# Laying the second pass's buffers in layers over the first's in a two-pass attention and FFN kernel, and interleaving the work at the seam

## What is computed

```python
xn = _layernorm(x)
Q, K = elu(xn @ Wq + bq) + 1, elu(xn @ Wk + bk) + 1
KV = einsum('bshd,bshm->bhdm', K, v)
Z = 1 / (einsum('bshd,bhd->bsh', Q, K.sum(axis=1)) + EPS)
o = einsum('bshd,bhdm,bsh->bshm', Q, KV, Z)
x1 = _layer_norm(xn + o @ Wo + bo, g1, be1)
s = _layer_norm(x1 + gelu(x1 @ W1 + b1) @ W2 + b2, g2, be2)
h = silu(fp4_linear(xn, w_gate)) * fp4_linear(xn, w_up)
out = x + s * silu(fp4_linear(h, w_down))
```

## Time and profile before

| | us |
|---|---|
| median of 3 runs | 1816.92 (1813.23 to 1817.27) |
| the profiled execution, its own time | 1815.74 |
| its span, first to last instruction | 1813.9 |
| TensorE, VectorE, ScalarE, GpSimd busy | 1708.1, 1334.5, 969.1, 705.6 |
| chain that ended last, by engine | PE 76%, DVE 13%, issue 4%, DMA 2%, ACT 2% |

### The profile page before, as it was taken

How to read it: one execution, slowest core, us unless ns; L and a number is a source line. 1 busy time by engine, 2 the same in 40 slices (tenths; PEclk the granted TensorE clock), 3 DMA queues, 4 the chain that set the end, 5 groups by cost and what they waited for, 6 DMA issues and landing times.

```text
span 1813.9 us, 30486 instructions
## 1 busy us (share of the span) xinstructions
PE 1708.1 (94%) x11091; PEld 1515.0 (84%) x11091; DVE 1334.5 (74%) x2733; ACT 969.1 (53%) x1756; POOL 705.6 (39%) x518
## 2 busy tenths in 40 slices
PE   6888999999869999999999999999999999999997
PEld 4766778787659988898998989899898998989886
DVE  5575645646357879797787879788787978878794
ACT  5444555555334654646465464646556464655543
POOL 4443433333213434333434434343343334334344
PEclk9899999999979999999999999999999999999998
DMA  5311222312130010111101010110101021010100
GB/s 175 115 69 54 81 92 69 117 61 100 55 131 1 1 48 1 48 45 53 48 1 48 1 47 23 75 48 1 48 1 47 2 96 48 1 48 1 47 1 24
DMA packets 65946, 89.33 MB, mean 49 GB/s; under 512 B 4211, under 2 KB 50439, under 8 KB 64774
## 3 DMA queue, kind: packets, MB, share of 16 engines
q1 hardware_dynamic: 65798, 87.39, 14.2%
HBM read 53.29 MB, written 34.08 MB: 48 GB/s over the span
## 4 chain that ended last, share of the span: by engine, by line
PE 76%; DVE 13%; issue 4%; DMA 2%; ACT 2%; POOL 1%; SPq 1%; POOLq 0%; DVEq 0%; ACTq 0%
PE QH L77 9%; PE QH L79 9%; PE QH L78 9%; PE AC L77 8%; PE AC L79 8%; PE AC L78 8%; PE GU L77 4%; PE GU L79 4%; PE GU L78 4%; PE QH L696 2%; PE DN L77 2%; PE DN L79 2%; PE DN L78 2%; PE TT L778 2%; DVE hb L1655 1%
## 5 line engine op out<-in xcount | busy, mean ns | idle before, releaser
L2102 POOL TENSOR_TENSOR hb<-hb,rs_h 128x704 f32<-128x704 f32 x64 | 89.0, 1391 | 322.4 <-DVE rs_h L1662 322.4
L1115 ACT ACTIVATE rh<-QH 128x512 fp32r<-128x512 f32 x256 | 150.3, 595 | 103.5 <-DVE QH L1790 101.9
L1805 DVE TENSOR_TENSOR rl<-QH,rh 128x512 fp32r<-128x512 f32 x128 | 85.2, 675 | 131.0 <-ACT rh L1115 103.6
L77 PE MATMUL GU<-wgh,xqh 128*128 128x352 f32 x448 | 148.4, 331 | 6.8 <-DVE hb L1655 5.2
L2107 POOL TENSOR_TENSOR hb<-hb,sn_h 128x704 f32<-128x704 f32 x64 | 89.1, 1392 | 165.1 <-DVE hb L1667 165.1
L1415 DVE SCALAR_TENSOR_TENSOR u<-ex,QH 128x512 f32<-128x512 f32 x128 | 84.9, 682 | 91.9 <-ACT ex L986 91.3
L77 PE MATMUL AC<-Mh,rh 128*128 128x256 f32 x512 | 146.5, 286 | 0.0
L78 PE MATMUL GU<-wgl,xqh 128*128 128x352 f32 x448 | 145.7, 325 | 0.0
L79 PE MATMUL GU<-wgh,xql 128*128 128x352 f32 x448 | 145.4, 324 | 0.0
L77 PE MATMUL AC<-w2h,rh 128*128 128x256 f32 x512 | 144.6, 282 | 0.0
L79 PE MATMUL AC<-Mh,rl 128*128 128x256 f32 x512 | 143.9, 281 | 0.0
(11 more groups left out here) (232 smaller groups left out, 5724.4 us busy)
## 6 DMA issues: line engine op xcount, KB each, us to landing
xa<-in_L_attn_src SPq DMA_DIRECT2D x16, 512.0 KB, 4.7
xt_scratch<-xth SPq DMA_DIRECT2D x32, 256.0 KB, 4.9
xt_scratch<-xtl SPq DMA_DIRECT2D x32, 256.0 KB, 5.0
xb<-in_L_attn_src SPq DMA_DIRECT2D x16, 512.0 KB, 4.1
xnTh<-xt_scratch SPq DMA_DIRECT2D x32, 256.0 KB, 4.6
xnTl<-xt_scratch SPq DMA_DIRECT2D x32, 256.0 KB, 5.4
out<-x SPq DMA_DIRECT2D x16, 512.0 KB, 6.5
m_scratch<-mh SPq DMA_DIRECT2D x16, 256.0 KB, 2.4
```

The costliest lines, as they stand in the source:

```text
L77: e.matmul(outp, lh, rh, start=start, stop=False, skip_group_check=check)
L1115: e.activation(RH[j % 4][:], src, ACT.Copy).then_inc(S[sem], 1)
L1805: e.tensor_tensor(RL[j % 4][:], QH[:, (j % 2) * 512:(j % 2 + 1) * 512], f(RH[j % 4][:]), ALU.subtract).then_inc(S["gel"], 1)
L2102: e.tensor_tensor(hb, hb, spread(rs_h[i % 2][:], 44), ALU.mult).then_inc(S["hin"], 1)
```

## The change

Nothing that is computed changes. The edits:

1. **Buffers.** The one scope A becomes three layers. The row buffers Xb[0], XN and the small am_x, sn_x, rs_x get bytes that only rawc and vrows used. xnTh, xnTl and xa (and dn_s, zhi) lie over `raw`, the buffer of the weight chain. The rest of the prologue's buffers (zd, sel, XC, HC, xqh, Q32, EG, HB, ksB, Mh, ...) lie over the buffers of the tiles. Those of the maps (gt, kvt, wo_s, mhl, ...) lie under Xb[1], x1, xTh, Gb, RH, RL, hqh. So `end_of_a` becomes three waits: `raw_done`, `main_done`, `maps_done`.
2. **Loads.** `load_xb(0)`, `load_xn(0)` and the six loads of row vectors go to tile 50 of SyncE's loop, behind `raw_done`. `load_m(0)` follows `main_done`, ahead of the stores of the last maps.
3. **Group 0's first steps.** `x_norm(0, 0..3)` go to ScalarE's tiles 58 to 61, `x_max` and `x_scale` of both pairs to VectorE's tiles 60 and 62, `x_in(0, 0)` to GpSimd's tile 61.
4. **The last maps** are written between the first Q products on TensorE, ScalarE and VectorE, all in bank DN (before, DN and TT in turn).
5. **GpSimd.** `x_plus_bo(0)` goes from ahead of `h_in(0)` to behind `h_out(1)` and `maps_done`.
6. **Weights' chain.** The parts 2 and 3 are quantised at tiles 26 and 28 (before, 14 and 20). Their turns are at 30 to 33 and 42 to 45 (before, 25 to 32). rawc no longer shares gt.
7. The loop's turn for g = 0 is written out, in the same order, and the loop begins at 1.

```diff
-        turn_at = {**{14 + n: n for n in range(4)}, **{25 + n: 4 + n for n in range(8)}}
-        quant_at = {10: 0, 12: 1, 14: 2, 20: 3}
+        turn_at = {14: 0, 15: 1, 16: 2, 17: 3, 30: 4, 31: 5, 32: 6, 33: 7, 42: 8, 43: 9, 44: 10, 45: 11}
+        quant_at = {10: 0, 12: 1, 26: 2, 28: 3}
...
+        def main_done(w):
+            w.wait_ge(S["A_G"], 2 * NT)
+            w.wait_ge(S["A_K"], 2 * NT)
+            w.wait_ge(S["A_xl"], NT)
+            w.wait_ge(S["xs0"], 32 * (NT // 4))
+            w.wait_ge(S["xs1"], 32 * (NT // 4))
+        def maps_done(w):
+            w.wait_ge(S["A_ksm"], NB)
+            w.wait_ge(S["A_M"], 4 * NB)
+            w.wait_ge(S["A_Mc"], 8 * NB)
+            w.wait_ge(S["A_mh"], 4 * NB)
+            w.wait_ge(S["A_ml"], 4 * NB)
+            w.wait_ge(S["A_ks"], 5 * NB)
+            w.wait_ge(S["kst"], 16 * NB)
+            w.wait_ge(S["m0"], 32 * 2 * NB)
+            w.wait_ge(S["m1"], 32 * 2 * NB)
+        def raw_done(w):
+            w.wait_ge(S["A_wT"], 12)
+            w.wait_ge(S["A_qp"], 4)
```

SyncE:

```diff
-                if i == 34:
+                if i == 50:
+                    raw_done(w)
+                    load_xb(0)
+                    load_xn(0)
...
-            w.wait_ge(S["A_k"], 2 * NT)
-            w.wait_ge(S["A_K"], 2 * NT)
-            e.dma_start(Xb[0][:], src_t[0]).then_inc(S["x0"], 16)
+            main_done(w)
+            load_m(0)
...
-            end_of_a(w)
...
-            load_xn(0)
-            load_m(0)
+            maps_done(w)
```

TensorE:

```diff
+            q_proj(0, 0)
             k_sums(NB - 1)
             kv_map(NB - 1, 0)
+            q_proj(0, 1)
             kv_map(NB - 1, 1)
-            for r in range(4):
-                m_map(NB - 1, r)
-            end_of_a(w)
...
-            q_proj(0, 0)
-            q_proj(0, 1)
             q_proj(0, 2)
             q_proj(0, 3)
+            m_map(NB - 1, 0)
+            m_map(NB - 1, 1)
             turn_xq(0, 0)
             q_proj(0, 4)
             q_proj(0, 5)
+            m_map(NB - 1, 2)
             gate_up(0, 1)
+            m_map(NB - 1, 3)
             q_proj(0, 6)
             q_proj(0, 7)
             gate_up(0, 0)
```

VectorE (ScalarE likewise: `m_hi` 0 to 3 between the `q_exp`, `maps_done` ahead of `z_hi(0, 0)`):

```diff
-            x_max(0, 0)
-            x_scale(0, 0)
+            k_sums(NB - 1)
             q_elu(0, 0)
             x_round(0, 0)
+            kv_out(NB - 1, 0)
             q_elu(0, 1)
-            x_max(0, 1)
+            kv_out(NB - 1, 1)
             q_elu(0, 2)
+            m_out(NB - 1, 0)
             q_elu(0, 3)
-            x_scale(0, 1)
+            m_lo(NB - 1, 0)
+            m_out(NB - 1, 1)
             xq_lo(0, 0)
+            m_lo(NB - 1, 1)
             q_elu(0, 4)
+            m_out(NB - 1, 2)
             q_elu(0, 5)
             x_round(0, 1)
+            m_lo(NB - 1, 2)
+            m_out(NB - 1, 3)
             gate_mul(0, 1)
+            m_lo(NB - 1, 3)
```

GpSimd:

```diff
-            end_of_a(w)
+            main_done(w)
...
-            x_in(0, 0)
             x_out(0, 0)
             x_in(0, 1)
             x_out(0, 1)
-            x_plus_bo(0)
             h_in(0)
             h_out(0)
             h_in(1)
             h_out(1)
+            maps_done(w)
+            x_plus_bo(0)
             ln1_rstd(0, 0)
```

More of the change, by code:

```diff
@@ new lines, in turn_h @@
+            def turn_h(i, hf):
+                g, t = i // 4, i % 4
+                w.wait_ge(S["hout"], i + 1)
+                w.wait_ge(S["hb0"], 3)
+                w.wait_ge(S["hTh"], 2 * i + hf)
+                w.wait_ge(S["hTl"], 2 * i + hf)
+                n = 2 * g + (3 if t == 3 and g + 1 < NG else 2)
+                w.wait_ge(S["xqTh"], n)
+                w.wait_ge(S["xqTl"], n)
+                for k in range(3):
+                    c = hf * HALF + k * 128
+                    last = e.transpose(TT[:, k * 128:(k + 1) * 128], HB[i % 3][:, c:c + 128], ident[:])
+                last.then_inc(S["hT"], 1)
@@ L1894, in _ @@
             gelu_lo(0, 5)
-            for g in range(NG):
+            gelu_lo(0, 6)
+            h_round(3)
+            h_lo(2, 0)
+            x_max(1, 0)
+            x_scale(1, 0)
+            gelu_lo(0, 7)
+            q_elu(1, 0)
+            x_round(1, 0)
+            q_elu(1, 1)
+            h_lo(2, 1)
+            g_mul(1)
+            ln_add("lnb", 0, 0)
+            ln_add("lnb", 0, 1)
+            x_max(1, 1)
+            q_elu(1, 2)
+            q_elu(1, 3)
+            x_scale(1, 1)
@@ new lines, in _ @@
+            ln_stats("lnb", 0)
+            xq_lo(1, 0)
+            q_elu(1, 4)
+            q_elu(1, 5)
+            x_round(1, 1)
+            g_mul(2)
+            gate_mul(4, 1)
+            q_elu(1, 6)
+            h_lo(3, 0)
+            q_elu(1, 7)
+            gate_mul(4, 0)
+            h_max(4)
+            den_inverse(1)
+            h_lo(3, 1)
+            z_parts(1)
+            gate_mul(5, 0)
+            h_scale(4)
+            gate_mul(5, 1)
+            xq_lo(1, 1)
+            z_mul(1, 0)
@@ new lines, in _ @@
+            z_mul(1, 1)
+            z_lo(1, 0)
+            z_lo(1, 1)
+            h_max(5)
+            z_mul(1, 2)
+            z_mul(1, 3)
+            gate_mul(6, 1)
+            z_lo(1, 2)
+            z_lo(1, 3)
+            h_round(4)
+            z_mul(1, 4)
+            z_mul(1, 5)
+            g_mul(3)
+            z_lo(1, 4)
+            z_lo(1, 5)
+            h_scale(5)
+            z_mul(1, 6)
+            z_mul(1, 7)
+            h_lo(4, 0)
+            z_lo(1, 6)
+            z_lo(1, 7)
@@ new lines, in _ @@
+            gate_mul(6, 0)
+            h_round(5)
+            h_lo(4, 1)
+            ln1_add(1, 0)
+            ln1_stats(1, 0)
+            ln1_add(1, 1)
+            ln1_stats(1, 1)
+            ln1_norm(1, 0)
+            ln1_norm(1, 1)
+            gate_mul(7, 0)
+            h_lo(5, 0)
+            xT_half(1, 0, "x1T", "x1Th", "x1Tl")
+            xT_half(1, 1, "x1T", "x1Th", "x1Tl")
+            final_add(0)
+            g_mul(4)
+            gate_mul(7, 1)
+            h_lo(5, 1)
+            h_max(6)
@@ L2174, in _ @@
             h_out(2)
-            for g in range(NG):
+            x_in(1, 0)
+            x_out(1, 0)
+            h_out(3)
+            x_in(1, 1)
+            ln_rstd("lnb", 0)
+            x_out(1, 1)
+            x_plus_bo(1)
+            h_in(4)
+            x2_affine(0)
+            h_out(4)
+            h_in(5)
+            final_mul(0)
+            h_out(5)
+            ln1_rstd(1, 0)
+            ln1_rstd(1, 1)
+            h_in(6)
+            h_in(7)
+            x1_residual(1)
+            h_out(6)
+            for g in range(1, NG):
                 a, b, c, d = 4 * g, 4 * g + 1, 4 * g + 2, 4 * g + 3
```

1078 lines of the change are left out of this document (605 added, 473 removed).

## The result

The changed kernel takes 1794.52 us (median of four runs, 1789.76 to 1800.31) against 1817.10 for the kernel before (four runs, 1813.23 to 1817.39): ratio 0.9882, 95% interval 0.9849 to 0.9915. A second measurement gave 1796.44 against 1814.49, ratio 0.9904 (0.9887 to 0.9921). So 18 to 23 us are gone. The forecast was 1801.5 within 1794 to 1810: the sign and the range hold, but the time lies at the low end.

A forecast was written before the change was run, and what follows sets the result against it. TensorE, nearly always busy in both passes, was taken to bound the kernel. 1815.7 - 22.4 + 0.5 + 3.1 + 1.5 + 2 = 1800.4; with the median 1.2 above the profiled execution, 1801.5 us, range 1794 to 1810.

The forecast's parts named there:

- The seam: Between the two passes: early rows and last maps laid between Q products, about 29.2 us from 478.7, gain 22.4.
- my layout: Step-by-step order of TensorE's work between the passes, from 478.7 until gate_up(0, 0) ends at about 508.1, before 530.5.
- x_plus_bo(0): GpSimd step behind h_out(1): ln1_add(0, 0) starts 3.1 us later, uncovered; +3.1, and +1.5 for the clock.
- The first rival: At turn_x1(0, 0): TensorE has the 3.1 us to spare, x_plus_bo is covered, total 1797; chance 0.15.
- The chain: Weights' turns and quantising in the first pass: 6 to 8 us go, 8 to 10 come, net +2 (-4 to +7).
- The mechanism: First pass: two consecutive turns stall TensorE when no K product lies between them; 3.18 us at tile 16's turn.
- The rival of 1827.5: First pass: VectorE and GpSimd fall behind at tiles 26 to 33 and 42 to 45, K comes late; chance 0.03.
- The collision at tiles 28 and 29: VectorE and GpSimd share a port pair: quant_round(2) at tile 29 waits for quant_in(3), an estimated 1.3 us more.
- Group 0's first steps: Steps moved to the end of the first pass lie mostly in idle ScalarE and VectorE time; 0 to 1 us, taken as +0.5.
- what would make the forecast wrong: First pass growing by more than 10 us, or new SBUF places changing an instruction's duration, for which no reason was seen.

The follow-up runs named there:

- the first pair: Changed kernel against the same with x_plus_bo(0) back ahead of h_in(0); the latter took 1790.66 us, ratio 0.9868 to the kernel before.
- the faster kernel: Changed kernel with x_plus_bo(0) ahead of h_in(0), turns spaced so none follows another without a K product between, part 3 quantised at tile 30: 1778.12 us, ratio 0.9813.

## Why the prediction came out as it did

**The seam: right, 28.6 us for 29.4.** Gain 51.8 - 28.6 = 23.2 instead of 22.4. The order was read off step by step: k_sums ended within 0.1 of its place after 478.7, kv_map(0) took 3.65 for the 3.4 of the lower clock that I had kept, m_map(1) waited 0.96 for the 0.9, gate_up(0, 0) waited 0.40 for VectorE. Taking back the early load loses 10.5 of it, taking back the interleaving 11.9. (The last step of my layout, 505.9 plus a gate_up of 1.9, gives 507.8 and not 508.1; it changes nothing.) maps_done opened early enough: the last store of the maps was issued at 512.19 and SyncE's load behind it at 515.11, and TensorE had no wait that traces to it.

**x_plus_bo(0): the wait right, the price right.** 3.50 for the 3.4, no cover. With the clock behind it I had 3.1 + 1.5 = 4.6. By the medians it was 5.8 and 2.4 when undone in the new layout, and 4.5 when added to before. By the traces it was 5.2 to 5.7 in the first pair. Over all profiled executions of the new layout, the four with the step early took 60.0 to 61.3 from g_out to turn_x1, mean 60.4, and 1247.2 to 1248.2 from there to the end, mean 1247.8. Those with it late took a mean of 64.0 (three with the whole seam) and 1249.3 (five), so 3.6 and 1.5. The first rival falls.

**The chain: right in sum, by terms that aren't all right.** I took +2, between -4 and +7; it is about 2.7 over eleven profiled executions. By stretches, forecast and the profiled pair: tiles 14 to 17 about 32.5, measured 30.2; 26 to 29 26 to 28, measured 29.8; 30 to 33 about 33, measured 30.6 (27.6 in the second execution); 42 to 45 about 27.5, measured 27.6. I also hadn't counted that tiles 18 to 25 become 2.9 shorter without turn 4 in them and with quantising gone from tile 20. The mechanism (a turn behind a turn) held at tiles 16, 32 and 44, as it did before at tiles 28 and 32 (1.97 us each), and the faster kernel is built on it. At tile 31 it was quant_round(3) instead, which I had named too. The rival of 1827.5 is out: the first pass grew by about 3 us, not by 26.

The collision at tiles 28 and 29 came, but with another victim. VectorE and GpSimd of after:

```profile
240.84 2.59 POOL L2278 TENSOR_TENSOR raw<-raw,rs_w 128x1408 f32<-128x1408 f32 x1
...
241.09 2.90 DVE L1563 TENSOR_TENSOR kal<-u,kah 128x512 fp32r<-128x512 f32 x1
...
246.14 0.96 DVE L1606 SCALAR_TENSOR_TENSOR raw<-rawc,raw 128x768 f32<-128x768 f32 x1
...
244.13 0.47 PE L77 MATMUL AC<-kah,xnh 128*128 128x512 f32 x1 [0.98 <-DVE kal L1563]
```

k_lo takes 2.90 us, where the m_lo of the same form takes 0.69, and ends 0.56 after quant_in(3). Before it took 2.28 and ended 0.54 after quant_in(1). The rule of the Trainium skill ("SBUF — State Buffer", section "SBUF: two separate sides"), that the pair of ports is held for a whole instruction, agrees with both. But my estimate put its 1.3 us on the wrong instruction: quant_round(2) comes later, and its second half takes 0.96. TensorE lost 0.98 to k_lo, and 2.10 at 247.84 waiting for VectorE's u, where I had expected something like the 2.62 of tiles 12 and 13.

**Group 0's first steps: nothing seen.** I took 0.5. They stand at tiles 58 to 62, and from tile 58 to g_out it takes 37.2 us, before 37.2 and 37.1. Tiles 46 to 57, ahead of them, are 0.3 to 0.6 longer, with the new loads at tile 50; why they are longer was not looked into.

**What failed: the rest of the sum, 5 to 7 us by the medians.** In the profiled pair the sum came out as 1800.4 for 1800.31, but that is luck: this execution had more matmuls at the lower clock up to tile 13 (126.6 us, 122.0 in the next), where nothing of the change lies. By the medians the gain was 18 to 23 us, not 15.4. Row by row of the table: from g_out to turn_x1 -20.0 where the terms say -22.4 + 3.1 = -19.3; tiles 14 to 57 +3.1 for +2.5 (the 2.7, and 0.4 in tiles 46 to 57); from turn_x1 to the end -1.0, where I had +1.5. That last row is the step that failed. The late x_plus_bo(0) cost its 1.5 there; without it the row is 1247.8 us, 2.7 less than before. Of that 1.7 to 2.6 lies in the groups 1 to 15, which I had called unchanged. Between the first and the last x_plus_bo of those groups the nine profiled executions of the new layout took 1118.2 to 1118.9, the three of the old one 1120.6 to 1120.8, all with a mean clock of 1.00. I had seen no reason for the new SBUF places to change a duration, and had named it as what would make the forecast wrong. The durations did change. TensorE by line over these groups, before and then after (busy, mean ns):

```profile
L78 PE MATMUL AC<-Ml,rh 128*128 128x256 f32 x448 | 125.9, 281 | 0.0
...
L78 PE MATMUL AC<-w2l,rh 128*128 128x256 f32 x448 | 125.0, 279 | 0.0
L78 PE MATMUL QH<-xnTl,wqh 128*128 128x512 f32 x224 | 88.4, 395 | 0.0
...
L78 PE MATMUL QH<-xTl,w1h 128*128 128x512 f32 x224 | 88.4, 394 | 0.0
```

```profile
L78 PE MATMUL AC<-w2l,rh 128*128 128x256 f32 x448 | 126.6, 283 | 0.0
L78 PE MATMUL AC<-Ml,rh 128*128 128x256 f32 x448 | 125.1, 279 | 0.0
...
L78 PE MATMUL QH<-xnTl,wqh 128*128 128x512 f32 x224 | 88.5, 395 | 0.0
L78 PE MATMUL QH<-xTl,w1h 128*128 128x512 f32 x224 | 87.7, 391 | 0.0
```

Some products are up to 1% faster, others up to 1.4% slower, and further executions of either layout show the same (Ml 281 and 278, w2l 279 and 283, w1h 394 and 392). These durations overlap, so their sums say nothing of the time. Counted from the start of one matmul to the start of the next, without waits, the products with M take 2.7 us less, those with w1 2.0, gate and up 1.6 and the Q products 0.4 less, and those with w2 2.4, those with w_down 1.6 and those of zd and sel 1.1 more. With 0.2 less of waits that is the 1.8 of this pair. Why this is so is open: the places are what differs for these instructions, but no run here moved a single buffer. Together the rows give -20.0 + 3.1 - 1.0 = -17.9; the remaining 0.1 to 4.7 us of the medians' 18 to 23 are, as far as the traces show, in what varies between executions of one kernel, the matmuls at the lower clock above all.

## What to carry over

A standstill behind a load at a seam is won twice, in its own time and in the matmuls at the lower clock behind it, and here it took two edits: the early load, and independent work laid between the dependent steps. Without the first 10.5 us were lost again, without the second 11.9. An operation moved behind others on an in-order engine costs its whole duration where the next consumer had no slack, and the wait of 0.3 us that stood there showed it; here no buffer even asked for the move. Before trusting one profiled execution to a few us, compare stretches of a second: where TensorE's busy time differs between two executions of one kernel, look at the granted clock first.

## What was not expected of the hardware

- The same kernel took 1789.76 to 1800.31 us in four runs, and the mean granted clock of each tells its place: 0.989 for the fastest, 0.986 for the two of 1793.34 and 1795.70, 0.982 for the slowest. The kernel before spread over 4.2 us in its first four runs and 11.6 in 13 others.
- A wait of 3.50 us was followed by a stretch at 1.2 GHz (0.88 over 13.8 us); the same place with a wait of 0.28 had none (1.00).
- Mean matmul durations differed between two layouts of the same buffers (279 to 283 ns, 1.4% more; 394 to 391 ns, 0.8% less), with no wait at them and the clock at 1.00.
- Beside GpSimd's quant_in VectorE's k_lo took 2.90 us instead of 0.69, and ended 0.56 us after it.
